# Landing tiles and the place of the high part in the last feed-forward of a transformer kernel

## The chip, the cores and the metric

The kernel runs on one core of a Trainium2 chip. The metric is the device time of one execution in microseconds (us); less is better. The engines are called PE (TensorE), DVE (VectorE), ACT (ScalarE), POOL (GpSimd) and SP (SyncE); each works through a queue of its own in order, and they wait for each other by semaphores.

## The reference

Input x is 8 x 1024 x 256 in float32. Four residual sublayers follow one another, each on a layer norm of x over the 256 features:

```
x = x + attention(layernorm(x))          # 2 heads of 128, rotary, causal softmax
x = x + ffn(layernorm(x))
x = x + linear_attention(layernorm(x))   # 8 heads of 64, decayed state, gated
x = x + ffn(layernorm(x))

ffn(x): gate = x @ (w_gate/127).T ; up = x @ (w_up/127).T      # 256 -> 768, integer weights
        return (silu(gate) * up) @ (w_down/127).T              # 768 -> 256
```

The change concerns the last line, the second use of ffn.

## The kernel before

x stays in the on-chip memory for the whole program (tile X, 64 tiles of 128 tokens). The program has four phases: attention, feed-forward 1 (ff1), linear attention, feed-forward 2 (ff2). Both feed-forwards come from one function, `feed_forward_phase` (line 954), called with nth = 1 or 2. Matmuls take operands that are split into a high part (rounded to float32r) and a low part (what is left), each used in a matmul of its own.

A feed-forward works in 16 units of 512 tokens. A unit has six steps f = 0 to 5, one for each 128 hidden features. In step f PE makes the gate projection (four matmuls 128x512, L1169) and the up projection (four more), then the down projection of the step three before (eight matmuls 128x256, L1178), which for f < 3 belongs to the unit before. ACT makes silu of the gate (L1106) and the high part of h of the step before (L1094). DVE makes h = silu * up (L1141), the low part of h of the step before (L1125), and besides: at f = 0 the statistics for the unit after next, at 1 their aggregation (L140), at 2 the residual of the unit before (L1132), at 3 the normalise of the unit after next (L156, four tiles), at 4 its block transpose (L256, `dve_blocks`).

The normalised units must be transposed for PE. DVE's block transpose turns squares of 32 x 32, and SP then moves the squares to their places with sixteen DMAs (`sp_move`, L271) into a landing tile. ACT makes the high part of what has landed (`act_high`, L276), POOL the low part (`pool_low`, L281), and PE waits for the low part (`pe_wait`) before the last down projection of the unit ahead. So in unit u: DVE normalises and transposes blocks of unit u + 2, SP moves unit u + 1, ACT and POOL make the two parts of unit u + 1. High and low parts have two tiles each, for even and odd units (`front.parts`: ln_xh, ln_xl and ff_odd_xh, ff_odd_xl). The landing tile is one, `raw`, in both feed-forwards. The tile of the blocks (ln_xn, upper half) is one too: DVE's transpose of unit u + 2 waits until unit u + 1 has landed (L255).

The order on each engine is written out by hand in the four functions `unit(u, par, first, left)`; par is the parity of the unit, `left` is 2 while two or more units follow, 1 in unit 14, 0 in unit 15. A `Signal` counts; `at(turn, k)` is the value after k events of that turn, and `at(u, 0)` is thus what the turn before has reached. SP's waits ahead of a move are, at line 1040 and in `sp_move`:

```
wait_alone(sp, front.lo_done.sem, front.lo_done.at(u, 1), front.sp_passed)
wait_alone(sp, self.blocks_done.sem, self.blocks_done.at(unit, 1), self.sp_passed)
```

On SP, after the move of unit u + 1, ff2 stores the result of unit u - 1 to memory (`store`, L1053). PE waits for h of three steps ago before a gate projection (three PSUM banks each for gate and up) and for the low part of a step before its down projection (`ready_for`, `down`). The chip runs the branch with terms = 2: the low parts of the integer weights are zero.

Of the kernel before, what the change touches and what calls it, by code (L numbers as in the profile page):

```python
# [13 lines left out]
F32 = mybir.dt.float32  # L14
# [7 lines left out]
P = 128  # L22
# [200 lines left out]
class Turned:  # L223
# [34 lines left out]

    def landing(self, par, raw):

        return self.raw[:] if raw else self.parts[par][1][:].bitcast(F32)

    def sp_move(self, sp, unit, par, raw=False):

        wait_alone(sp, self.blocks_done.sem, self.blocks_done.at(unit, 1), self.sp_passed)
        lo = self.landing(par, raw)
        for r in range(NQ):
            for c in range(NQ):
                src = self.blocks[r * SQ:(r + 1) * SQ, c, :].rearrange("p (n b) -> p n b", b=SQ)
                dst = lo[c * SQ:(c + 1) * SQ].rearrange("p k (t r b) -> p (k t) r b", t=UT, r=NQ)[:, :, r, :]  # L270
                sp.dma_start(dst, src).then_inc(self.landed.sem, 16)  # L271

    def act_high(self, act, unit, par, raw=False):
        hi, lo = self.parts[par]
        act.wait_ge(self.landed.sem, self.landed.at(unit, 16 * MOVES))
        self.nc.scalar.activation(hi[:], self.landing(par, raw), ACT.Copy).then_inc(self.hi_done.sem, 1)  # L276

    def pool_low(self, pool, unit, par, raw=False):
        hi, lo = self.parts[par]
        pool.wait_ge(self.hi_done.sem, self.hi_done.at(unit, 1))  # L280
        self.nc.gpsimd.tensor_tensor(lo[:], self.landing(par, raw), hi[:].bitcast(F32),  # L281
                                     ALU.subtract).then_inc(self.lo_done.sem, 1)
# [670 lines left out]
def feed_forward_phase(nc, block, sems, env, io, name, nth, front, following, signals):  # L953
# [5 lines left out]
    with ExitStack() as ctx:  # L959
# [21 lines left out]
        sx = [front.pair(0), front.pair(1)]  # L981
        NH = 4
        h_hi, h_lo = sb("h_hi", [P, NH, UN], F32R), sb("h_lo", [P, NH, UN], F32R)
        LAG = 3

        prep_hi, prep_lo = signals.prep_hi, signals.prep_lo
# [42 lines left out]
        @block.sync  # L1029
        def _(sp):  # L1030

            def unit(u, par, first, left):
                upcoming = next_of(u, par, left)
                if upcoming:
                    nfront, nu, npar = upcoming
                    if left:
                        if first:
                            sp.wait_ge(*env["a_scores_end" if nth == 1 else "lin_decayed_end"])
                        else:
                            wait_alone(sp, front.lo_done.sem, front.lo_done.at(u, 1), front.sp_passed)  # L1040
                    else:
                        wait_alone(sp, up_ready.sem, up_ready.at(u - 1, NF), front.sp_passed)
                    nfront.sp_move(sp, nu, npar, raw=bool(left))
                if following and isinstance(u, int) and u == 1:
                    sp.wait_ge(prep_lo, 2)
                    load_lin_weights(sp, env, io)
                if not following and not first:
                    store(u - 1)

            def store(u):  # L1050
                wait_alone(sp, x_done.sem, x_done.at(u, 1), front.sp_passed)
                at = bass.ds(u * UT, UT)
                sp.dma_start(out_v[:, at, :], X[:, at, :]).then_inc(stored, 16)  # L1053

            run_units(sp, unit, 1)
            if not following:
                store(NU - 1)
                sp.wait_ge(stored, 16 * NU)

        @block.gpsimd  # L1060
        def _(pool):

            def unit(u, par, first, left):
                upcoming, after = next_of(u, par, left), after_next(u, left)
                if first and nth == 1:
                    pool.wait_ge(*env["a_out_end"])
                    nc.gpsimd.tensor_copy(w_lo, stage[:, 0:NW]).then_inc(prep_lo, 2)
                if first and nth == 2:
                    pool.wait_ge(*env["lin_decayed_end"])
                    raw, hi = stage[:, parts_of_w[2]], w_hi[:, parts_of_w[2]]  # L1070
                    for f in range(NF):
                        at = slice(f * M, (f + 1) * M)
                        last = nc.gpsimd.tensor_tensor(lo_of_down[:, at], raw[:, at], hi[:, at].bitcast(F32), ALU.subtract)
                    last.then_inc(prep_lo, 1)
                if after and not first:
                    after[0].ln.pool_rstd(pool, after[1])
                if upcoming:
                    nfront, nu, npar = upcoming
                    nfront.pool_low(pool, nu, npar, raw=bool(left))

            def lin_low(n):
                at = bass.ds(n * LIN_PIECE, LIN_PIECE)
# [7 lines left out]
        def _(act):  # L1090
# [5 lines left out]
            def unit(u, par, first, left):  # L1096
                upcoming = next_of(u, par, left)
                for f in range(NF):
                    if f == (2 if first else NF - 2) and upcoming:
                        nfront, nu, npar = upcoming  # L1100
                        if left and not first:
                            act.wait_ge(up_ready.sem, up_ready.at(u - 1, NF))
                        nfront.act_high(act, nu, npar, raw=bool(left))
                    act.wait_ge(gate_ready.sem, gate_ready.at(u, f + 1))
                    act.wait_ge(h_done.sem, h_done.at(u, f - NB_GU + 1))
                    nc.scalar.activation(silu[:, f % NB_GU, :], PS[:, f % NB_GU, :], ACT.Silu,  # L1106
# [723 lines left out]
```

## Time and profile before

| | us |
|---|---|
| median of 3 runs | 1916.81 (1914.27 to 1918.74) |
| the profiled execution, own time | 1915.64 |
| its span | 1913.9 |
| granted TensorE clock, mean share | 0.998 |

The page gives for each engine its busy time in the span; the timelines give single instructions with start, length, engine, line, operation and, in brackets, how long the engine had been idle before and what it waited for. Starts count from the span's start. ff2's projections on PE run from 1618 us to the end.

### The profile page before, as it was taken

How to read it: one execution, taken by the hardware profiler on the slowest of the kernel's cores; microseconds unless marked ns; L12 is line 12 of the kernel's file. 1: busy time of each engine (PE TensorE's matmuls, PEld its weight loads, DVE VectorE, ACT ScalarE, POOL GpSimd, SP SyncE). 2: the span in 40 equal slices, each digit the busy share in tenths (PEclk: the TensorE clock that was granted, in tenths of full speed). 3: DMA queues.
4: the chain of work that ended last, by engine and by line, in shares of the span. 5: the costliest groups of instructions: out<-in, count | busy, mean ns of one | idle time of the engine just before them, and what ended most of it. 6: DMA issues, size and time to landing. Idle time of an engine off the chain costs nothing.

```text
span 1913.9 us, 36549 instructions
## 1 busy us (share of the span) xinstructions
PE 1875.6 (98%) x12321; PEld 1620.0 (85%) x12321; DVE 1325.4 (69%) x3141; ACT 879.4 (46%) x1716; POOL 519.6 (27%) x453
## 2 busy tenths in 40 slices
PE   7999999999999999999999999999999999899998
PEld 6888888888788888888888888888888887788887
DVE  6666566655677888766666666676667677778885
ACT  6666656665644444453333333333333332444443
POOL 5313202320321232132322222222222223422210
PEclk9999999999999999999999999999999999999999
DMA  7100000000022112220000000000000001222332
GB/s 251 33 1 0 0 0 0 0 0 0 12 63 46 29 29 32 34 66 12 13 10 10 9 9 9 10 11 11 11 11 11 12 12 18 38 62 62 64 59 53
DMA packets 230614, 53.19 MB, mean 28 GB/s; under 512 B 209680, under 2 KB 228752, under 8 KB 230160
## 3 DMA queue, kind: packets, MB, share of 16 engines
q1 hardware_dynamic: 229280, 49.53, 12.8%
q10 hardware_dynamic: 1264, 2.76, 0.4%
q8 instruction: 39, 0.64, 0.1%
q14 instruction: 31, 0.25, 0.0%
HBM read 18.69 MB, written 8.39 MB: 14 GB/s over the span
## 4 chain that ended last, share of the span: by engine, by line
PE 89%; DVE 4%; issue 2%; SPq 2%; POOL 1%; ACT 1%; DMA 0%; ACTq 0%; DVEq 0%; POOLq 0%
PE PS L323 18%; PE PS L1169 16%; PE PS L1178 9%; PE PS L332 7%; PE PS L855 7%; PE PS L826 6%; PE PS L1633 5%; PE PS L1675 4%; PE PS L1619 3%; PE PS L844 3%; PE PS L1652 3%; PE PS L866 2%; PE PS L1639 2%; SPq L271 2%; PE PS L1607 1%
## 5 line engine op out<-in xcount | busy, mean ns | idle before, releaser
L323 PE MATMUL PS<-ln_xh,lin_w 128*128 128x512 f32 x768 | 248.8, 392 | 0.0
L1106 ACT ACTIVATE ff_silu<-PS 128x512 f32<-128x512 f32 x192 | 114.5, 597 | 235.2 <-PE PS L1169 207.1
L1390 POOL TENSOR_TENSOR lin_yg_lo<-stage,lin_yg_hi 128x512 fp32r<-128x512 f32 x64 | 82.3, 1286 | 484.1 <-ACT lin_yg_hi L1408 484.1
L1141 DVE SCALAR_TENSOR_TENSOR ff_h<-PS,ff_silu 128x512 f32<-128x512 f32 x192 | 131.3, 685 | 111.3 <-PE PS L1169 93.5
L1408 ACT ACTIVATE lin_yg_hi<-stage 128x512 fp32r<-128x512 f32 x64 | 40.5, 632 | 347.0 <-DVE stage L1503 315.7
L323 PEld LDWEIGHTS PS<-ln_xh,lin_w 128*128 128x128 f32 x768 | 144.2, 188 | 28.7
L1125 DVE TENSOR_TENSOR ff_h_lo<-ff_h,ff_h_hi 128x512 fp32r<-128x512 f32 x192 | 168.2, 876 | 0.4
L564 POOL TENSOR_TENSOR qk<-qk,swapped 64x128 f32<-64x128 f32 (+2 forms) x96 | 96.5, 1005 | 243.0 <-DVE swapped L708 237.2
L1465 DVE TENSOR_TENSOR lin_AD<-PS,lin_decay 128x512 f32<-128x512 f32 x128 | 82.2, 684 | 104.6 <-PE PS L1619 104.6
L855 PE MATMUL PS<-probT,v_a 128*128 128x128 f32 x1152 | 153.4, 278 | 0.0
L855 PEld LDWEIGHTS PS<-probT,v_a 128*128 128x128 f32 x1152 | 139.5, 192 | 14.4 <-ACT probT L628 7.4
L323 PE MATMUL PS<-ln_xl,lin_w 128*128 128x512 f32 x384 | 150.0, 391 | 0.0
L826 PE MATMUL PS<-qk 128*128 128x512 f32 (+3 forms) x384 | 145.1, 489 | 0.9 <-POOL qk L564 0.9
L718 DVE TENSOR_REDUCE neg_max<-PS 128x1 f32<-128x256 f32 (+7 forms) x128 | 95.7, 753 | 64.3 <-PE PS L829 62.9
L1633 PE MATMUL PS<-lin_v,lin_AD 128*128 128x65 f32 x1024 | 133.4, 273 | 2.2 <-DVE lin_y L1478 2.2
L1633 PEld LDWEIGHTS PS<-lin_v,lin_AD 128*128 128x128 f32 x1024 | 124.2, 191 | 8.4 <-DVE lin_AD L1465 2.3
L1094 ACT ACTIVATE ff_h_hi<-ff_h 128x512 fp32r<-128x512 f32 x192 | 119.5, 623 | 10.9 <-DVE ff_h L1141 10.9
L167 POOL TENSOR_SCALAR ln_var_eps<-ln_mean_var 128x4 f32<-128x4 f32 x64 | 14.7, 229 | 360.4 <-DVE ln_mean_var L140 360.4
L1493 DVE SCALAR_TENSOR_TENSOR lin_state<-lin_state,lin_decay_c,PS 64x65 f32<-64x65 f32 x384 | 107.5, 280 | 7.0 <-PE PS L1652 2.9
L1178 PE MATMUL PS<-lin_w,ff_h_hi 128*128 128x256 f32 x384 | 97.9, 288 | 7.8 <-issue 5.8
L1178 PE MATMUL PS<-ff_w_hi,ff_h_hi 128*128 128x256 f32 x384 | 97.9, 288 | 4.4 <-DVE ff_h_lo L1125 1.9
L618 ACT ACTIVATE prob<-PS,neg_max 128x256 f32<-128x256 f32 (+7 forms) x128 | 94.5, 738 | 14.6 <-DVE neg_max L718 11.5
(172 smaller groups left out, 5183.8 us busy)
## 6 DMA issues: line engine op xcount, KB each, us to landing
ff_raw<-ln_xn SPq DMA_DIRECT2D x480, 32.0 KB, 2.0
ln_xl<-ln_xn SPq DMA_DIRECT2D x288, 32.0 KB, 1.9
out_x<-X SPq DMA_DIRECT2D x16, 512.0 KB, 2.9
X<-in_x SPq DMA_DIRECT2D x7, 1024.0 KB, 5.5
stage<-in_w_lin SPq DMA_DIRECT2D x1, 2048.0 KB, 8.2
stage<-in_w_gate SPq DMA_DIRECT2D x2, 768.0 KB, 7.4
stage<-in_w_up SPq DMA_DIRECT2D x2, 768.0 KB, 8.9
stage<-in_w_down SPq DMA_DIRECT2D x2, 768.0 KB, 10.2
```

What stands on the lines that cost most here:

```text
L323: last = nc.tensor.matmul(out, w, x, start=n == 0, stop=n == len(terms) - 1)
L332: last = nc.tensor.matmul(out, x[:, at], w, start=n == 0, stop=n == len(terms) - 1)
L826: last = nc.tensor.matmul(bank[:, 0:w], qk[:, 0, h, i * P:(i + 1) * P], qk[:, 1, h, c:c + w], start=True, stop=not diag)
L855: last = nc.tensor.matmul(O, V[:, j, h * DA:(h + 1) * DA], probT[:, n % 2, j, :], start=j == 0, stop=j == i)
L1094: nc.scalar.activation(h_hi[:, slot(par, f), :], h[:, f % 2, :], ACT.Copy).then_inc(hi_done.sem, 1)
L1106: nc.scalar.activation(silu[:, f % NB_GU, :], PS[:, f % NB_GU, :], ACT.Silu, scale=W_SCALE).then_inc(silu_done.sem, 1)
L1125: nc.vector.tensor_tensor(h_lo[:, slot(par, f), :], h[:, f % 2, :], h_hi[:, slot(par, f), :].bitcast(F32), ALU.subtract).then_inc(lo_done. ...
L1141: nc.vector.scalar_tensor_tensor(h[:, f % 2, :], PS[:, NB_GU + f % NB_GU, :], W_SCALE, silu[:, f % NB_GU, :], ALU.mult, ALU.mult).then_inc ...
L1169: ins = nc.tensor.matmul(PS[:, bank, :], w, x, start=n == 0, stop=n == len(parts) - 1)
L1178: ins = nc.tensor.matmul(Y[:, t // 2, (t % 2) * M:(t % 2 + 1) * M], a[:, slot(par, f), t * P:(t + 1) * P], w[:, f % NF, :], start=f == 0 a ...
L1493: last = nc.vector.scalar_tensor_tensor(S[rows, j, cols], S[rows, j, cols], Gc[rows, j:j + 1], new, ALU.mult, ALU.add)
L1633: last = nc.tensor.matmul(bank[:, hh * VA:(hh + 1) * VA], AD[:, ch % 2, hh % 2, 2 * g + hh // 2, :], v[:, c, HG * g + hh, :], start=hh == ...
```

## The change

In ff2 alone (nth = 2) a second landing tile raw2 is added; even units land in it, odd ones in raw. SP's first wait ahead of a move asks for the low part of unit u - 1 in place of unit u (`at(u, 2 - nth)`). ACT makes the high part of the next unit at step NF - 1 - nth, which is 3 in place of 4; in ff1 it is 4 as before. With the high part, POOL's low part is released a step sooner. Unit 0 keeps its step 2, and its SP wait is of another kind and stays.

```diff
--- before.py
+++ after.py
@@ -258,9 +258,9 @@
 
     def landing(self, par, raw):
 
-        return self.raw[:] if raw else self.parts[par][1][:].bitcast(F32)
-
-    def sp_move(self, sp, unit, par, raw=False):
+        return self.parts[par][1][:].bitcast(F32) if raw is None else raw
+
+    def sp_move(self, sp, unit, par, raw=None):
 
         wait_alone(sp, self.blocks_done.sem, self.blocks_done.at(unit, 1), self.sp_passed)
         lo = self.landing(par, raw)
@@ -270,12 +270,12 @@
                 dst = lo[c * SQ:(c + 1) * SQ].rearrange("p k (t r b) -> p (k t) r b", t=UT, r=NQ)[:, :, r, :]
                 sp.dma_start(dst, src).then_inc(self.landed.sem, 16)
 
-    def act_high(self, act, unit, par, raw=False):
+    def act_high(self, act, unit, par, raw=None):
         hi, lo = self.parts[par]
         act.wait_ge(self.landed.sem, self.landed.at(unit, 16 * MOVES))
         self.nc.scalar.activation(hi[:], self.landing(par, raw), ACT.Copy).then_inc(self.hi_done.sem, 1)
 
-    def pool_low(self, pool, unit, par, raw=False):
+    def pool_low(self, pool, unit, par, raw=None):
         hi, lo = self.parts[par]
         pool.wait_ge(self.hi_done.sem, self.hi_done.at(unit, 1))
         self.nc.gpsimd.tensor_tensor(lo[:], self.landing(par, raw), hi[:].bitcast(F32),
@@ -981,6 +981,7 @@
         sx = [front.pair(0), front.pair(1)]
         NH = 4
         h_hi, h_lo = sb("h_hi", [P, NH, UN], F32R), sb("h_lo", [P, NH, UN], F32R)
+        raws = (sb("raw2", [P, KT, UN]), front.raw) if nth == 2 else (front.raw, front.raw)
         LAG = 3
 
         prep_hi, prep_lo = signals.prep_hi, signals.prep_lo
@@ -1037,10 +1038,10 @@
                         if first:
                             sp.wait_ge(*env["a_scores_end" if nth == 1 else "lin_decayed_end"])
                         else:
-                            wait_alone(sp, front.lo_done.sem, front.lo_done.at(u, 1), front.sp_passed)
+                            wait_alone(sp, front.lo_done.sem, front.lo_done.at(u, 2 - nth), front.sp_passed)
                     else:
                         wait_alone(sp, up_ready.sem, up_ready.at(u - 1, NF), front.sp_passed)
-                    nfront.sp_move(sp, nu, npar, raw=bool(left))
+                    nfront.sp_move(sp, nu, npar, raw=raws[npar][:] if left else None)
                 if following and isinstance(u, int) and u == 1:
                     sp.wait_ge(prep_lo, 2)
                     load_lin_weights(sp, env, io)
@@ -1076,7 +1077,7 @@
                     after[0].ln.pool_rstd(pool, after[1])
                 if upcoming:
                     nfront, nu, npar = upcoming
-                    nfront.pool_low(pool, nu, npar, raw=bool(left))
+                    nfront.pool_low(pool, nu, npar, raw=raws[npar][:] if left else None)
 
             def lin_low(n):
                 at = bass.ds(n * LIN_PIECE, LIN_PIECE)
@@ -1096,11 +1097,11 @@
             def unit(u, par, first, left):
                 upcoming = next_of(u, par, left)
                 for f in range(NF):
-                    if f == (2 if first else NF - 2) and upcoming:
+                    if f == (2 if first else NF - 1 - nth) and upcoming:
                         nfront, nu, npar = upcoming
                         if left and not first:
                             act.wait_ge(up_ready.sem, up_ready.at(u - 1, NF))
-                        nfront.act_high(act, nu, npar, raw=bool(left))
+                        nfront.act_high(act, nu, npar, raw=raws[npar][:] if left else None)
                     act.wait_ge(gate_ready.sem, gate_ready.at(u, f + 1))
                     act.wait_ge(h_done.sem, h_done.at(u, f - NB_GU + 1))
                     nc.scalar.activation(silu[:, f % NB_GU, :], PS[:, f % NB_GU, :], ACT.Silu,
```

How the order moves on ACT, in ff2, unit 2 (first the silu of a step, L1106, then the high part of h of the step before, L1094; L276 is the high part of the next unit). Before:

```order
736 L1106 ACTIVATE ff_silu<-PS 128x512 [waits ff2_h_done,ff2_gate_ready]
737 L1094 ACTIVATE ff_h_hi<-ff_h 128x512 [waits ff2_down_done,ff2_h_done]
738 L1106 ACTIVATE ff_silu<-PS 128x512 [waits ff2_h_done,ff2_gate_ready]
739 L1094 ACTIVATE ff_h_hi<-ff_h 128x512 [waits ff2_down_done,ff2_h_done]
740 L276 ACTIVATE ff_odd_xh<-ff_raw 128x1024 [waits ff2_landed,ff2_up_ready]
741 L1106 ACTIVATE ff_silu<-PS 128x512 [waits ff2_h_done,ff2_gate_ready]
742 L1094 ACTIVATE ff_h_hi<-ff_h 128x512 [waits ff2_down_done,ff2_h_done]
```

After the change:

```order
736 L1107 ACTIVATE ff_silu<-PS 128x512 [waits ff2_h_done,ff2_gate_ready]
737 L1095 ACTIVATE ff_h_hi<-ff_h 128x512 [waits ff2_down_done,ff2_h_done]
738 L276 ACTIVATE ff_odd_xh<-ff_raw 128x1024 [waits ff2_landed,ff2_up_ready]
739 L1107 ACTIVATE ff_silu<-PS 128x512 [waits ff2_h_done,ff2_gate_ready]
740 L1095 ACTIVATE ff_h_hi<-ff_h 128x512 [waits ff2_down_done,ff2_h_done]
741 L1107 ACTIVATE ff_silu<-PS 128x512 [waits ff2_h_done,ff2_gate_ready]
742 L1095 ACTIVATE ff_h_hi<-ff_h 128x512 [waits ff2_down_done,ff2_h_done]
```

L276 stood between the high part of step 2 and the silu of step 4; it now stands one pair sooner, ahead of the silu of step 3.

DVE's order in ff2 is the same before and after but for line numbers one higher. Here it is before, in the second unit of the loop's body, from h of step 3 to the transpose of the unit after next:

```order
1075 L1141 SCALAR_TENSOR_TENSOR ff_h<-PS,ff_silu 128x512 [waits ff2_h_lo_done,ff2_silu_done,ff2_up_ready]
1076 L1125 TENSOR_TENSOR ff_h_lo<-ff_h,ff_h_hi 128x512 [waits ff2_down_done,ff2_h_hi_done]
1077 L156 TENSOR_SCALAR ln_xn<-X,ln_mean_var,ln_rstd 128x8x32 [waits ff2_ln_rstd_done]
1078 L156 TENSOR_SCALAR ln_xn<-X,ln_mean_var,ln_rstd 128x8x32 x3
1079 L1138 REGISTER_ALU
1080 L1141 SCALAR_TENSOR_TENSOR ff_h<-PS,ff_silu 128x512 [waits ff2_h_lo_done,ff2_silu_done,ff2_up_ready]
1081 L1125 TENSOR_TENSOR ff_h_lo<-ff_h,ff_h_hi 128x512 [waits ff2_down_done,ff2_h_hi_done]
1082 L255 ISA [waits ff2_ln_ready]
1083 L256 STREAM_TRANSPOSE ln_xn<-ln_xn 128x1024 [waits ff2_landed]
```

Nothing moved here; between h of step 3 and the transpose stand a low part, the normalise, h of step 4 and another low part.

## Rows read from the trace of the kernel before

**Rows 1.** The page: span and busy time by engine.
```profile
span 1913.9 us, 36549 instructions
...
PE 1875.6 (98%) x12321; PEld 1620.0 (85%) x12321; DVE 1325.4 (69%) x3141; ACT 879.4 (46%) x1716; POOL 519.6 (27%) x453
```

**Rows 2.** Chain that ended last, unit 15: start us, us, what.
```profile
1887.83 1.84 PE PS L1169 x8
...
1901.80 1.84 PE PS L1169 x8
```

**Rows 3.** Timeline of PE, starts of units 2, 7 and 8: start us, us, engine, line.
```profile
1662.77 0.40 PE L1169 MATMUL PS<-ln_xh,lin_w 128*128 128x512 f32 x1
...
1749.34 0.40 PE L1169 MATMUL PS<-ff_odd_xh,lin_w 128*128 128x512 f32 x1
...
1766.49 0.40 PE L1169 MATMUL PS<-ln_xh,lin_w 128*128 128x512 f32 x1
```

**Rows 4.** Timeline of ACT, 1756 to 1780 us; in brackets idle before.
```profile
1756.55 0.62 ACT L1094 ACTIVATE ff_h_hi<-ff_h 128x512 fp32r<-128x512 f32 x1
...
1761.83 1.06 ACT L276 ACTIVATE ln_xh<-ff_raw 128x1024 fp32r<-128x1024 f32 x1 [1.86 <-DMA ff_raw<-ln_xn]
1762.80 0.58 ACT L1106 ACTIVATE ff_silu<-PS 128x512 f32<-128x512 f32 x1
...
1778.91 1.06 ACT L276 ACTIVATE ff_odd_xh<-ff_raw 128x1024 fp32r<-128x1024 f32 x1 [1.80 <-DMA ff_raw<-ln_xn]
```

**Rows 5.** Timeline of DVE, 1763 to 1780 us.
```profile
1763.46 0.69 DVE L1141 SCALAR_TENSOR_TENSOR ff_h<-PS,ff_silu 128x512 f32<-128x512 f32 x1 [1.12 <-PE PS L1169]
1764.07 1.85 DVE L1125 TENSOR_TENSOR ff_h_lo<-ff_h,ff_h_hi 128x512 fp32r<-128x512 f32 x1
1765.84 1.23 DVE L256 STREAM_TRANSPOSE ln_xn<-ln_xn 128x1024 f32<-128x1024 f32 x1
...
1774.72 0.68 DVE L1125 TENSOR_TENSOR ff_h_lo<-ff_h,ff_h_hi 128x512 fp32r<-128x512 f32 x1
...
1778.11 1.38 DVE L156 TENSOR_SCALAR ln_xn<-X,ln_mean_var,ln_rstd 128x256 f32 x4
```

**Rows 6.** Timeline of POOL, unit 7.
```profile
1762.97 2.40 POOL L281 TENSOR_TENSOR ln_xl<-ff_raw,ln_xh 128x1024 fp32r<-128x1024 f32 x1 [5.67 <-ACT ln_xh L276]
```

**Rows 7.** Timeline of SP, the move of unit 9.
```profile
1767.17 10.40 SPq L271 DMA_DIRECT2D ff_raw<-ln_xn  x16
```

**Rows 8.** Waits of SP, 1732 to 1852 us (seven units): us, times, longest.
```profile
SPq L83 <- POOL ff_odd_xl L281: 15.3, 4, 4.0
SPq L83 <- POOL ln_xl L281: 12.2, 3, 4.1
SPq L83 <- DVE ln_xn L256: 11.1, 7, 1.6
```

**Rows 9.** Timelines of SP, DVE, POOL and ACT, units 0 to 2.
```profile
1618.97 35.52 SPq L271 DMA_DIRECT2D ff_raw<-ln_xn  x32
...
1635.83 1.23 DVE L256 STREAM_TRANSPOSE ln_xn<-ln_xn 128x1024 f32<-128x1024 f32 x1
...
1640.84 2.33 POOL L281 TENSOR_TENSOR ff_odd_xl<-ff_raw,ff_odd_xh 128x1024 fp32r<-128x1024 f32 x1
...
1657.49 3.54 DVE L156 TENSOR_SCALAR ln_xn<-X,ln_mean_var,ln_rstd 128x256 f32 x4
...
1676.12 1.06 ACT L276 ACTIVATE ff_odd_xh<-ff_raw 128x1024 fp32r<-128x1024 f32 x1 [2.72 <-PE PS L1169]
```

**Rows 10.** Timelines of ACT and PE, end of unit 14.
```profile
1882.99 1.06 ACT L276 ACTIVATE ff_odd_xh<-ff_raw 128x1024 fp32r<-128x1024 f32 x1 [1.86 <-DMA ff_raw<-ln_xn]
...
1886.64 0.36 PE L1178 MATMUL PS<-lin_w,ff_h_hi 128*128 128x256 f32 x1 [0.16 <-issue]
```

**Rows 11.** Busy time by stretch; columns to PEclk, the granted clock.
```profile
1639.00:1643.30 4.30, 0.12 (x2) 0.06 (x1) 4.17 (x4) 0.63 (x1) 4.17 (x4) 1.00 0.00 0
1643.30:1648.00 4.70, 4.70 (x19) 3.98 (x20) 0.42 (x1) 1.11 (x2) 0.00 (x0) 0.64 0.23 34
```

## The prediction

> **What bounds the kernel now.** I read the page first. TensorE (PE) is busy 98% of the span [rows 1]. A reader could stop there and call the kernel PE-bound. In the last feed-forward (ff2) that is nearly true and not quite, and the difference decides this case, so I went on to the timelines of the engines.
>
> PE's own pace comes from unit 15, which has no next unit to prepare. From its first to its last step 13.97 us pass for five steps [rows 2], 2.79 us a step, so six steps are 16.77 us. But unit 7 starts at 1749.34 and unit 8 at 1766.49 [rows 3]: 17.15 us. Something slower than PE sets the pace of the inner units by about 0.4 us.
>
> It is a closed loop through the other engines. Follow one turn from start to start. ACT makes the high part of unit 8 at 1761.83, having stood 1.86 us for the landing, and the silu of step 4 starts 0.97 later, at 1762.80 [rows 4]. DVE's product h of step 4 starts 0.66 later, at 1763.46; the low part of step 3 0.61 later; the block transpose (L256) of the unit after next 1.77 later, at 1765.84 [rows 5]. SP begins its sixteen DMAs 1.33 after that, at 1767.17, and issues them for 10.40 us [rows 7]. ACT takes the next landing at 1778.91 [rows 4], 1.34 after the last issue. The sum is 0.97 + 0.66 + 0.61 + 1.77 + 1.33 + 10.40 + 1.34 = 17.08 us. There is no slack in it: each member starts when the one before allows it. The low part takes 1.85 us there and 0.68 elsewhere [rows 5], because POOL's low part of the next unit runs from 1762.97 to 1765.37 [rows 6].
>
> **The change part by part.** The first feed-forward, attention and linear attention keep their instructions: for nth = 1 both index formulas give the old numbers and both landings are the same tile. Cost nothing. The added tile takes memory and no instruction. Every count of instructions stays (16 moves per unit, one high and one low part).
>
> *SP's weaker wait.* SP no longer waits for the low part of unit u, only for that of u-1, before it waits for the blocks. The view of SP's waits says what this is worth: seven times SP waited for POOL's low part and then, all seven times, 11.1 us in total, 1.59 us more each for DVE's transpose [rows 8]. The blocks are always last, and the blocks are not sooner by this edit. So in the steady units it is worth nothing. There is one exception. At the start SP issued two moves in a stretch that ends at 1654.49 [rows 9]; the second, 10.40 long, thus began at about 1644.1, since it waited for POOL's low part of unit 1 (1640.84 + 2.33 = 1643.17), though its blocks were done at 1637.06. It can now begin at 1637.2, 6.9 us sooner. ACT then finds unit 2 landed at step 3 of unit 1, POOL is done before DVE's normalise there, and that takes 1.38 us [rows 5] instead of the 3.54 it took while POOL ran [rows 9]. Against this DVE's low part, just before, is held some 0.3 us. The first fully exposed landing (ACT at 1676.12 [rows 9]) comes about 1.8 us sooner: -1.8 us.
>
> *The high part a step sooner.* This is the dear part. On ACT the high part now stands ahead of the silu of step 3. Were its data there, it would be free: in the unit that starts at 1749.34 ACT has done the work ahead of it by 1757.17 (7.83 us into the unit), but the landing is taken at 1761.83 (12.49 into it) [rows 3, 4]. ACT takes its queue in order, so it waits, and what queues behind it is now the silu of step 3, the high part of step 2, and everything DVE makes of them. The added members of the loop are those DVE has in order between h of step 3 and h of step 4. The new turn, from the start of the high part: silu of step 3 (0.97), h of step 3 (0.66), low part of step 2 (0.61), which meets POOL at the same offset as now and so is held alike (1.77), then the normalise of four tiles (1.38, less 0.07 of overlap: 1.31), h of step 4 (0.61 to the next start), low part of step 3 unheld (0.60: 0.68 less overlap), transpose to SP (1.33), 10.40, 1.34. That is 17.08 + 1.31 + 0.61 + 0.60 = 19.60 us, 2.52 more. The silu and high part that h and low part of those steps want are ready: ACT ends them some 2.6 and 3.2 us after the high part starts, and DVE comes to h of step 4 at 5.3.
>
> Can a head start save it? Only at first: landing 3, at 1676.12 - 1.8 = 1674.3, comes 11.5 us into unit 2, which starts at 1662.77 [rows 3], and ACT would be free at 7.8, so it waits already. Each turn takes 19.60 while PE would turn in some 17, so the lateness grows by 2.5 us a unit, and within two or three units PE itself stands at the end of step 5. There it needs the next unit's low part (1.14 + 2.40 us after the high part starts) and the low part of h of step 2, which ends 0.97 + 0.66 + 0.61 + 1.85 = 4.09 us after it. The second is later, by 0.5 us. PE's other waits are met: h of step 4 is done 6.0 us after the high part starts, and PE wants it at 4.1 + 0.1 + 1.05 (down projection) + 1.84 (first projections of the next unit [rows 2]) = 7.1. From then on the pace is the loop's.
>
> From the exposed landing at 1676.12 [rows 9] to the last at 1882.99 [rows 10] there are twelve turns: 12 x 2.52 = +30.2 us. Before, PE went on 3.65 us after the last landing (1886.64 [rows 10]); now 4.2: +0.5. The sum is 30.2 + 0.5 - 1.8 = +28.9 us.
>
> *The clock of PE.* Each unit now holds a pause of 19.6 - 16.8 = 2.8 us. After the pause of 4.2 us that ended at 1643.3 the granted clock was 0.64 over the next 4.7 us [rows 11], a part of it at 1.2 GHz instead of 2.4: 0.36 x 4.7 = 1.7 us lost. If every pause cost this, PE would still reach the end of step 5 1.1 us before it may go on. I count 0; the upper bound is in the range through the dearer case.
>
> The Trainium skill ("Trainium Kernel Development and Optimization", Best Practices) says to double-buffer so that DMA overlaps compute. By that rule the second landing tile lengthens the time in which a transfer may lie beside work, and the time would be that of the faster rival below; by the row of SP's waits [rows 8] the landing tile is not what SP waits for last. The row decides.
>
> **The sum.** The profiled execution took 1915.64 us (span 1913.9), so 1944.5 by its terms. It is 1.2 below the median of the three runs shown, 1916.81; between the two, I say 1945.0.
>
> **The rivals.**
>
> *Cheaper loop (0.12).* If the low part of step 2 were not held by POOL, the turn would be 1.17 shorter: 12 x (2.52 - 1.17) + 0.5 - 1.8 = +15 us, 1931. Against it: POOL starts 1.14 us after the high part, the low part of h 2.24 after it, in the new order as in the old [rows 4 to 6]. The Trainium skill ("SBUF — State Buffer", the section on its two separate sides) says the port pair that VectorE and GpSimd share is held by one of them for a whole instruction, the other blocked; by that this rival is out.
>
> *Dearer loop (0.13).* The normalise too meets POOL (3.54 for 1.38 [rows 5, 9], +2.16, less what the low part then saves, 1.17), or the pauses' slower clock delays gates that a silu waits for. One such microsecond a turn is +12 us, 1957.
>
> *Faster (0.07).* The loop is opened: the landing comes before ACT wants it, so high and low part lie under steps 3 and 4, POOL no longer holds the low part ahead of the transpose, and PE runs at its own pace. Then thirteen units save up to 0.38 us each (17.15 - 16.77), 5 us: 1912. This is what happens if landings come by 7.8 us into a unit. For it: the transpose would come about 1.8 us sooner once POOL is out of its way, as in unit 1. Against it: the landing stands at 12.5, the ten microseconds of issue stay, and landing 3 with all the head start still comes at 11.5.
>
> *No change (0.04).* DVE's idle time swallows the added members, and the turn stays at 17.1. DVE does stand 1.12 us before h of step 4 [rows 5], but it stands there because ACT and PE are not further; time before the landing does not shorten what comes after it. 1917.
>
> **How the numbers follow.** The forecast itself has 0.64. A measurement of this kernel tells about 0.2% (4 us) from no change. Slower: 0.64 + 0.12 + 0.13 = 0.89. Same: 0.04. Faster by more than 0.2%: 0.07. The range reaches from just under the cheaper loop to the dearer one, 1929 to 1957; outside it are the faster and the unchanged case and a part of the dearer.
>
> **What would show it.** Right: in ff2 the L276 rows on ACT lie 19.6 us apart in place of 17.1, each with some 6 to 7 us of idle time before it put to the DMA; SP waits for the transpose alone, for longer; PE has a pause of 2 to 3 us a unit ahead of a down projection, put down to DVE's low part; the busy share of PE in the last fifth of the span falls to about 86%; units of ff1 keep 17.1. Wrong: L276 with no idle time before it, or turns at 17.1, would say that the loop was not the pace-setter; turns well over 20 us, that a wait was added which I do not have.

## The result and the profile after

| | before | after |
|---|---|---|
| median of 4 runs each, us | 1915.99 (1914.27 to 1918.74) | 1944.01 (1942.90 to 1944.97) |
| span of the profiled execution, us | 1913.9 | 1941.4 |
| granted TensorE clock, mean share | 0.998 | 0.994 |

The ratio after to before is 1.0148, with a 95% interval of 1.0136 to 1.0160: 28 us slower. Line numbers of the changed kernel are one higher than before from the new line on. The page of the kernel after, its span, busy times and the chain by engine and by line, answers to [rows 1].

```profile
span 1941.4 us, 36549 instructions
...
PE 1883.1 (97%) x12321; PEld 1626.4 (84%) x12321; DVE 1318.3 (68%) x3141; ACT 878.0 (45%) x1716; POOL 523.8 (27%) x453
...
PE 80%; DVE 6%; SPq 6%; issue 3%; DMA 1%; ACT 1%; POOL 1%; ACTq 0%; DVEq 0%; POOLq 0%
```

The counts of instructions are those of before. The page alone says little, since 97% in place of 98% for PE would hardly alarm anyone. The chain does: SP's queue now has 6% of the whole span and PE 80%. The chain line of the page before reads:

```profile
PE 89%; DVE 4%; issue 2%; SPq 2%; POOL 1%; ACT 1%; DMA 0%; ACTq 0%; DVEq 0%; POOLq 0%
```

In the stretch from 1700 to 1760 us alone, the chain of the kernel after has no matmul in it at all. This is its summary by line:

```profile
by line: SPq L271 46.8%; issue 13.5%; DVE ff_h_lo L1126 12.5%; DMA ff_raw<-ln_xn 9.7%; DVE ln_xn L256 7.8%; DVE ln_xn L156 5.7%; ACT ff_silu L1107 2.9%; DVE ff_h L1142 0.8%; DVEq L1139 0.4%; DVEq L1141 0.2%; ACTq L1094 0.2%; ACTq L1106 0.1%
```

The same stretch of the kernel before is PE alone:

```profile
by line: PE PS L1169 64.4%; PE PS L1178 35.9%; issue 0.0%
```

In this stretch the loop through ACT, DVE and SP is now the only thing that sets the pace. Here is one turn of it. ACT's timeline after, 1750 to 1772 us, answers to [rows 4]:

```profile
1752.00 1.06 ACT L276 ACTIVATE ff_odd_xh<-ff_raw 128x1024 fp32r<-128x1024 f32 x1 [6.50 <-DMA ff_raw<-ln_xn]
1752.97 0.58 ACT L1107 ACTIVATE ff_silu<-PS 128x512 f32<-128x512 f32 x1
...
1771.60 1.06 ACT L276 ACTIVATE ln_xh<-ff_raw 128x1024 fp32r<-128x1024 f32 x1 [5.05 <-DMA ff_raw<-ln_xn]
```

DVE's timeline after, same turn ([rows 5]):

```profile
1753.63 0.69 DVE L1142 SCALAR_TENSOR_TENSOR ff_h<-PS,ff_silu 128x512 f32<-128x512 f32 x1 [5.90 <-ACT ff_silu L1107]
1754.24 1.81 DVE L1126 TENSOR_TENSOR ff_h_lo<-ff_h,ff_h_hi 128x512 fp32r<-128x512 f32 x1
1755.98 1.37 DVE L156 TENSOR_SCALAR ln_xn<-X,ln_mean_var,ln_rstd 128x256 f32 x4
1757.27 0.68 DVE L1142 SCALAR_TENSOR_TENSOR ff_h<-PS,ff_silu 128x512 f32<-128x512 f32 x1
1757.88 0.67 DVE L1126 TENSOR_TENSOR ff_h_lo<-ff_h,ff_h_hi 128x512 fp32r<-128x512 f32 x1
1758.47 1.23 DVE L256 STREAM_TRANSPOSE ln_xn<-ln_xn 128x1024 f32<-128x1024 f32 x1
```

SP's timeline after ([rows 7]):

```profile
1759.81 10.43 SPq L271 DMA_DIRECT2D ff_raw<-ln_xn  x16
```

From 1752.00 to 1771.60 pass 19.60 us. The normalise, one h and one low part now stand between the landing and the transpose. What used to be a wait of ACT of 1.86 us for the landing is 5.0 to 6.5 us in these units. The view of waits after, 1700 to 1850 us (us, times, longest), shows who stands for it; the last line is SP's own queue, 1732 to 1852 us ([rows 8]):

```profile
DVE ff_h L1142 <- ACT ff_silu L1107: 38.4, 7, 5.9
...
ACT ff_odd_xh L276 <- DMA ff_raw<-ln_xn: 24.5, 4, 6.5
...
ACT ln_xh L276 <- DMA ff_raw<-ln_xn: 23.1, 4, 6.5
...
PE PS L1179 <- DVE ff_h_lo L1126: 14.0, 7, 2.4
```

```profile
SPq L83 <- DVE ln_xn L256: 47.6, 6, 8.1
```

SP waited 38.6 us in seven units before the change, 27.5 of them put to POOL; now it waits 47.6 in six units, all for the transpose. Freed of one wait, it stands longer in the next.

### The profile page after: what moved, and what is told of

The parts are those of the page before. It is cut to its first block, busy times and chain, and to the rows that moved or that the text cites. A ratio compares the mean times of both kernels' runs of the same rounds, so it can differ in the third digit from the quotient of the medians.

```text
span 1941.4 us, 36549 instructions
## 1 busy us (share of the span) xinstructions
PE 1883.1 (97%) x12321; PEld 1626.4 (84%) x12321; DVE 1318.3 (68%) x3141; ACT 878.0 (45%) x1716; POOL 523.8 (27%) x453
## 3 DMA queue, kind: packets, MB, share of 16 engines
q1 hardware_dynamic: 229280, 49.53, 12.6%
## 4 chain that ended last, share of the span: by engine, by line
PE 80%; DVE 6%; SPq 6%; issue 3%; DMA 1%; ACT 1%; POOL 1%; ACTq 0%; DVEq 0%; POOLq 0%
PE PS L323 18%; PE PS L1170 10%; PE PS L332 7%; PE PS L855 7%; PE PS L826 6%; SPq L271 6%; PE PS L1179 6%; PE PS L1634 5%; PE PS L1676 4%; PE PS L1620 3%; PE PS L844 3%; PE PS L1653 3%; PE PS L866 2%; DVE ff_h_lo L1126 2%; PE PS L1640 2%
## 5 line engine op out<-in xcount | busy, mean ns | idle before, releaser
L1179 PEld LDWEIGHTS PS<-lin_w,ff_h_hi 128*128 128x128 f32 x384 | 75.1, 196 | 43.6 <-issue 15.3
```

Of the source, the lines that this page charges most:

```text
L1179: ins = nc.tensor.matmul(Y[:, t // 2, (t % 2) * M:(t % 2 + 1) * M], a[:, slot(par, f), t * P:(t + 1) * P], w[:, f % NF, :], start=f == 0 a ...
```

## The experiments

Each kernel below was timed beside the kernel before on the same chip; ratios are to it. "Turn" is the distance from one L276 of ff2 to the next on ACT, in the stretch from 1715 to 1790 us.

**Two tiles alone.** The change, with the high part back at step 4.

```diff
-                    if f == (2 if first else NF - 1 - nth) and upcoming:
+                    if f == (2 if first else NF - 2) and upcoming:
```

> Two landing tiles and SP's weaker wait alone; the high part stays at step 4 in ff2. My theory (the pace of a unit is the loop transpose, sixteen DMAs, high part, silu, h, low part, transpose; 17.08 us before, 19.60 after): SP's removed wait never ended last in the steady units, so turns between high parts (L276) stay at 17.1 us and the time is that of before within 0.2% (-2 to +1 us, ratio 0.999 to 1.0005). Rival (the tiles or the earlier DMAs cost time, or the landings collide with other work): ratio near 1.015, turns over 18 us. Rival (two tiles free the loop): turns under 16.95 us, 4 to 5 us faster.

Measured: 1915.40 us beside 1915.22, ratio 1.0001 [0.9991, 1.0010]. ACT's timeline of this kernel:

```profile
1744.03 1.06 ACT L276 ACTIVATE ff_odd_xh<-ff_raw 128x1024 fp32r<-128x1024 f32 x1 [1.84 <-DMA ff_raw<-ln_xn]
1761.16 1.06 ACT L276 ACTIVATE ln_xh<-ff_raw 128x1024 fp32r<-128x1024 f32 x1 [1.84 <-DMA ff_raw<-ln_xn]
```

The turn is 17.1 and the wait for the landing 1.84, both as before. With the high part at its old step, the second tile and the weaker wait are worth nothing that the interval of 0.1% to either side could tell. The rule to double-buffer that the prediction weighed (the Trainium skill, "Trainium Kernel Development and Optimization", Best Practices) has no gain to show here, for in the steady units the buffer was not what a transfer waited for last.

**The step alone.** The kernel before, one landing tile, old wait, with the high part at step 3.

```diff
-                    if f == (2 if first else NF - 2) and upcoming:
+                    if f == (2 if first else NF - 1 - nth) and upcoming:
```

> One landing tile and SP's old wait; the high part at step 3 in ff2. My theory: the whole loss is here, turns 19.6 us, PE pauses of about 2.5 us a unit, and the time is +28 to +31 us on before (ratio 1.0145 to 1.0165), as slow as the full change or up to 2 us slower. Rival (the loss comes from the second tile): no slower than before.

Measured: 1944.88, ratio 1.0150 [1.0133, 1.0167]. On ACT:

```profile
1755.51 1.06 ACT L276 ACTIVATE ff_odd_xh<-ff_raw 128x1024 fp32r<-128x1024 f32 x1 [5.01 <-DMA ff_raw<-ln_xn]
1775.11 1.06 ACT L276 ACTIVATE ln_xh<-ff_raw 128x1024 fp32r<-128x1024 f32 x1 [6.50 <-DMA ff_raw<-ln_xn]
```

A turn of 19.60 again. The loss is the step's: its ratio is that of the full change (1.0148) within the intervals, and the tiles alone stood at 1.0001.

**The normalise out of the loop.** The change, with ff2's normalise at DVE's step 2 instead of 3, so that it lies ahead of the landing.

```diff
-                        if f == (1 if first else 3):
+                        if f == (1 if first else 4 - nth):
```

> The full change, and in ff2 DVE normalises the unit after next at step 2 in place of 3, so that the normalise (1.31 us from start to start) leaves the loop. My theory: turns 19.60 - 1.31 = 18.3 us, twelve of them give back 15.7 us: about +12 us on before (ratio 1.006 to 1.007). Rival (the loss is ACT's wait as such, 6.5 us of idle in front of the high part, whatever DVE has between): turns stay at 19.6 us, ratio 1.015.

Measured: 1931.89, ratio 1.0088 [1.0071, 1.0105], 12.1 us less than the change. DVE's timeline, from h of step 3 on:

```profile
1750.67 0.69 DVE L1142 SCALAR_TENSOR_TENSOR ff_h<-PS,ff_silu 128x512 f32<-128x512 f32 x1 [3.56 <-issue]
1751.28 1.84 DVE L1126 TENSOR_TENSOR ff_h_lo<-ff_h,ff_h_hi 128x512 fp32r<-128x512 f32 x1
1753.25 0.69 DVE L1142 SCALAR_TENSOR_TENSOR ff_h<-PS,ff_silu 128x512 f32<-128x512 f32 x1
```

The turn is 18.53, where taking out 1.31 would give 18.29, and the ratio lies above the 1.006 to 1.007 that I had expected. The missing 0.24 stands in these rows: from the start of the held low part to the next member were 1.74 us in the change and are 1.97 here. That next member is now h, which has a semaphore wait on the low part that has just been made, and no other work lies between to cover it. That a member taken out gives back its length less what it covered is my reading of these rows; no run tests it by itself. The rival, a turn that stays at 19.6, is out: the normalise is a member of the loop.

**The transpose first.** The kernel before; in ff2 DVE transposes the blocks ahead of the low part of h in step 4, not behind it.

```diff
+                    if after and not first and f == 4 and nth == 2:
+                        after[0].dve_blocks(dve, after[1], (front, u + 1))
                     if f > 0 or not first:
                         low_part(u, par, f - 1)
...
-                        if f == (2 if first else 4):
+                        if f == (2 if first else 4) and (first or nth == 1):
```

> The kernel before, and in ff2 DVE's block transpose at step 4 goes ahead of the low part of step 3, which takes 1.77 us out of the loop: it could turn in 15.3 us, under PE's 16.8 to 16.9. My theory: turns fall to PE's pace, 16.8 to 17.0 us, and 2 to 5 us are gained (ratio 0.9975 to 0.999), less if the normalise now meets POOL's low part. Rival (PE sets the pace of before already): turns stay at 17.1, no gain.

Measured: 1910.81, ratio 0.9976 [0.9966, 0.9985]. A gain, from the same loop. Its turns alternate, 15.58 and 18.27. DVE's and then POOL's timeline, behind a landing that came at the end of a short turn (1758.52):

```profile
1759.57 3.60 DVE L156 TENSOR_SCALAR ln_xn<-X,ln_mean_var,ln_rstd 128x256 f32 x4
```

```profile
1759.66 2.39 POOL L281 TENSOR_TENSOR ln_xl<-ff_raw,ln_xh 128x1024 fp32r<-128x1024 f32 x1 [3.75 <-ACT ln_xh L276]
```

When a landing is in time, POOL's low part meets the normalise, whose four instructions then take 3.60 us in place of 1.38; the next transpose and landing are late by it, POOL then starts later and misses the normalise, and so on. The mean is 16.92 us.

Three more kernels ask what remains when the loop is short.

**The transpose first in both feed-forwards** (the edit above without its `nth` conditions).

> The kernel before, and the block transpose at step 4 ahead of the low part in both feed-forwards (the residual stays). My theory: ff1 has the same loop of 17.1 us as ff2 and gains about the same as ff2 did alone (4.4 us): 6 to 9 us faster than before, units of 16.9 us. Rival (ff1 is not bound by the loop): the 4.4 us of ff2 alone.

Measured: 1905.06, ratio 0.9948 [0.9933, 0.9964]. That is 10.4 us, a little more than the 6 to 9 expected. ff1 had the same loop: from its first landing taken from raw to the last pass 241.67 us here and 246.13 in the kernel before, 4.5 us less.

**The residual too.** In both feed-forwards, of the kernel before, residual and transpose ahead of the low part.

```diff
-                    if f > 0 or not first:
-                        low_part(u, par, f - 1)
                     if f == LAG - 1 and not first:
                         residual(u - 1, down_done.at(u, 0))
+                    if after and not first and f == 4:
+                        after[0].dve_blocks(dve, after[1], (front, u + 1))
+                    if f > 0 or not first:
+                        low_part(u, par, f - 1)
...
-                        if f == (2 if first else 4):
+                        if f == 2 and first:
```

> The kernel before, and on DVE in both feed-forwards the block transpose (step 4) and the residual (step 2) go ahead of the low part of that step. My theory: both loops run at PE's own pace, 16.77 us a unit, since PE no longer waits 0.15 us for the residual at step 3 nor for POOL at step 5: 0.36 us a unit in some 13 units of each of two feed-forwards, 8 to 11 us faster than before (ratio 0.9945 to 0.996). Rival (the low parts, later by 1.2 us, hold a down projection): turns over 17.1, no gain or slower.

Measured: 1902.85, ratio 0.9935 [0.9921, 0.9948]; the mean turn is 16.80 (its turns alternate too, 15.57 and 18.03). The gain of 12.6 us is above the 8 to 11 expected. The page hides why the residual matters. These are PE's first projection and its first matmul of the down projection in step 5 of unit 7 of the kernel before; the next unit starts at 1766.49 [rows 3]:

```profile
1763.45 0.40 PE L1169 MATMUL PS<-ff_odd_xh,lin_w 128*128 128x512 f32 x1
...
1765.43 0.39 PE L1178 MATMUL PS<-lin_w,ff_h_hi 128*128 128x256 f32 x1
```

In the kernel before PE is never idle in a unit, yet in step 3 of unit 7 the projections start 1.91 us ahead of the down projection, not 1.84, and that one takes 1.03 instead of 0.95: +0.15, the wait for the residual, gone here. In step 5 they read 1.98 and 1.06: +0.24, the wait for POOL's low part, which ends at 1765.37 [rows 6]. Together they are, to 0.01, the 0.38 by which a unit was above PE's own pace; with the transpose first 16.92 are left, with the residual too 16.80. The intervals of the kernel above (0.9948) and of this one (0.9935) overlap, so the residual's own share rests on the turns.

**Everything sooner.** The same order on DVE; in ff2 also the two tiles, the high part at step 3, the normalise at step 2 and the transpose at step 3.

> The order of b1 in ff1; in ff2 the full change (two landing tiles, high part at step 3) with DVE's side brought forward as well: normalise at step 2, transpose at step 3 ahead of the low part, residual ahead of the low part. My theory: the loop is then high part, silu, h, transpose, moves (15.3 us), so PE sets the pace in ff2 too and the high part at step 3 costs nothing: the time of b1 within 2 us. Rival (the high part at step 3 is dear in itself): slower than before.

Measured: 1909.59, ratio 0.9966 [0.9952, 0.9979], 6.7 us more than the kernel above: a miss. Its turn is 17.40. DVE's timeline:

```profile
1756.27 3.47 DVE L156 TENSOR_SCALAR ln_xn<-X,ln_mean_var,ln_rstd 128x256 f32 x4
...
1760.26 1.23 DVE L256 STREAM_TRANSPOSE ln_xn<-ln_xn 128x1024 f32<-128x1024 f32 x1
```

The high part a step sooner puts POOL's low part (1757.09, 2.50 us) right on the normalise in every unit of this stretch, and PE stands 0.40 us a unit for the low part of h behind it. So the place of the high part was undone alone:

**The same, with the high part back at step 4.**

```diff
-                    if f == (2 if first else NF - 1 - nth) and upcoming:
+                    if f == (2 if first else NF - 2) and upcoming:
```

> As the kernel with everything brought forward on DVE (ff2: two landing tiles, normalise at step 2, transpose at step 3, residual and transpose ahead of the low parts; ff1: transpose and residual ahead), but the high part of ff2 back at step 4. That kernel's turns were 17.4 us, with PE waiting 0.4 us a unit for the low part of step 2, behind the normalise that POOL's low part holds (3.47 us). My theory: with the high part a step later POOL's low part meets neither, and ff2 falls to PE's 16.8 us: the time of the kernel with only the DVE order changed (ratio 0.993 to 0.995). Rival (the loss against it comes from the normalise at step 2 or the transpose at step 3): ratio 0.9965 again.

Measured: 1901.66, ratio 0.9929 [0.9916, 0.9943], the lowest of all. This is 7 us below the kernel above by the ratios, so in this order too the high part costs something at step 3. ACT's timeline:

```profile
1733.19 1.05 ACT L276 ACTIVATE ff_odd_xh<-ff_raw 128x1024 fp32r<-128x1024 f32 x1
1749.97 1.05 ACT L276 ACTIVATE ln_xh<-ff_raw 128x1024 fp32r<-128x1024 f32 x1
1766.74 1.05 ACT L276 ACTIVATE ff_odd_xh<-ff_raw 128x1024 fp32r<-128x1024 f32 x1
```

DVE's timeline in the same unit:

```profile
1749.88 1.38 DVE L156 TENSOR_SCALAR ln_xn<-X,ln_mean_var,ln_rstd 128x256 f32 x4
...
1751.78 1.24 DVE L256 STREAM_TRANSPOSE ln_xn<-ln_xn 128x1024 f32<-128x1024 f32 x1
1752.93 1.14 DVE L1126 TENSOR_TENSOR ff_h_lo<-ff_h,ff_h_hi 128x512 fp32r<-128x512 f32 x1
```

POOL's and then SP's timeline:

```profile
1751.10 2.43 POOL L281 TENSOR_TENSOR ln_xl<-ff_raw,ln_xh 128x1024 fp32r<-128x1024 f32 x1 [3.69 <-ACT ln_xh L276]
```

```profile
1753.11 10.41 SPq L271 DMA_DIRECT2D ff_raw<-ln_xn  x16
```

No bracket stands behind L276: the landing is there before ACT wants it. The normalise is all but done as POOL starts (it ends 0.16 us later, at its 1.38), and only the end of POOL's work meets a low part of h; PE is at work in all of the 150 us from 1700 to 1850. The turn of 16.78 is PE's own pace. Here SP does use the second tile: its moves begin at 1753.11, while POOL reads the other tile until 1753.53. Yet the gain over one tile and the better order (0.9935) lies inside the intervals of both. With one tile this kernel's moves would start about 0.4 us later, and by my estimate still land some 1.5 us before ACT takes them (1753.53 + 10.41 + 1.34 = 1765.3 against 1766.74); no run tests that.

The last two kernels shorten the loop at its longest member, SP's issue, in the changed kernel.

**Half of the moves on ACT, in one piece.** SP issues eight of the sixteen, ACT the other eight behind the high part of its step 0 (ff2, units 1 to 14).

```diff
-            for c in range(NQ):
+            for c in cs:
...
+                    if nth == 2 and f == 0 and not first and left:
+                        nfront, nu, npar = upcoming
+                        wait_alone(act, front.lo_done.sem, front.lo_done.at(u, 0), act_passed)
+                        nfront.sp_move(act, nu, npar, raw=raws[npar][:], cs=range(2, NQ), passed=act_passed)
```

> The full change, and in ff2 units 1 to 14 SP issues eight of the sixteen moves and ACT the other eight, after the high part at step 0. My theory: the issue time of one queue, 10.40 us, is the largest member of the loop; halved, the loop could turn in 19.6 - 5.2 = 14.4 us, so PE sets the pace (16.8 to 17.0 us a unit) though the high part stands at step 3: 2 to 5 us faster than before (ratio 0.997 to 0.999), 32 us faster than the full change. Rival (the high part at step 3 costs by its place on ACT, not by the lateness of the landing): still 19 us or more a turn, ratio above 1.01. Second rival (5.2 us of DMA issue on ACT delays silu): turns between 17 and 19 us.

Measured: 1934.38, ratio 1.0095 [1.0080, 1.0111]. That is 9.6 us below the change, a part only of what the loop's arithmetic promised, and still slower than before: the second rival of the expectation came true. ACT's timeline:

```profile
1739.96 0.60 ACT L1109 ACTIVATE ff_silu<-PS 128x512 f32<-128x512 f32 x1 [1.75 <-PE PS L1176]
1740.42 0.61 ACTq L271 DMA_DIRECT2D ff_raw<-ln_xn  x1
...
1741.06 4.76 ACTq L271 DMA_DIRECT2D ff_raw<-ln_xn  x7
1746.00 0.60 ACT L1109 ACTIVATE ff_silu<-PS 128x512 f32<-128x512 f32 x1 [4.93 <-PE PS L1176]
...
1748.02 1.06 ACT L276 ACTIVATE ff_odd_xh<-ff_raw 128x1024 fp32r<-128x1024 f32 x1
```

and PE's long wait in the view of waits, 1700 to 1850 us:

```profile
PE PS L1185 <- DVE X L1139: 13.2, 8, 1.9
```

The landing is no longer late. But ACT cannot make the silu of step 1 while it issues: 6.04 us pass between two silus that PE feeds 2.79 apart. (The view puts the 4.93 us to PE, because issuing counts as idle; the rows between say what ACT did.) Through h and what DVE makes behind it, the residual last, this reaches PE as a pause of mostly 1.7 us, at most 1.9, and the turn is 18.7, which is 1.9 above PE's 16.8.

**The same moves on ACT, spread** as 3, 3 and 2 over its steps 0 to 2.

```diff
+                    if nth == 2 and f < 3 and not first and left:
...
+                        nfront.sp_move(act, nu, npar, raw=raws[npar][:], moves=range(8 + 3 * f, min(11 + 3 * f, MOVES)),
+                                       passed=act_passed, wait=f == 0)
```

> As the split of the moves before (the full change, eight moves on SP, eight on ACT in ff2 units 1 to 14), but ACT's eight are spread: three at step 0, three at step 1, two at step 2, so that no silu is held over 2 us. In the first split the turn was 18.7 us with no wait for the landing and a new wait of 1.7 us of PE for the residual, which I put down to ACT's five microseconds of issue in one piece. My theory: spread out, that wait goes, the landing comes by some 10.5 us into the unit, and the high part at step 3 costs nothing: units of 16.9 to 17.1 us, ratio 0.997 to 1.000. Rival (the issue of DMAs on ACT costs whatever its place, or the high part at step 3 does): turns over 18 us, ratio over 1.005.

Measured: 1909.87, ratio 0.9966 [0.9955, 0.9977]. ACT's timeline (the high part is L279 here):

```profile
1740.06 1.06 ACT L279 ACTIVATE ff_odd_xh<-ff_raw 128x1024 fp32r<-128x1024 f32 x1 [1.60 <-DMA ff_raw<-ln_xn]
...
1756.95 1.06 ACT L279 ACTIVATE ln_xh<-ff_raw 128x1024 fp32r<-128x1024 f32 x1 [1.58 <-DMA ff_raw<-ln_xn]
```

The turn is 16.89, and the change with this addition is 34 us below the change alone (1909.87 against 1944.01), though ACT still waits 1.6 us at step 3. So the step is not dear by itself; it is dear while the loop through SP's ten microseconds is longer than PE's unit. The Trainium skill ("Trainium Kernel Development and Optimization", Key Constraints) says that issuing DMAs from several engines saves only the issuing sequencer's time. Both runs agree, and that time, 5.41 us of SP's issue in place of 10.43, is what was wanted here: from issue to landing a move took 2.0 us in the median from SP and from ACT alike.

## Why the prediction was right

The forecast was 1945.0 us, the median is 1944.01, and the mechanism is the one that was forecast: the step, through the loop. The sum was made against the profiled execution, so its terms are compared with the profiled spans, 1913.9 and 1941.4. The landings that bound the stretches, on ACT's timeline after (the third and the last), answer to [rows 9] and [rows 10]:

```profile
1673.53 1.06 ACT L276 ACTIVATE ff_odd_xh<-ff_raw 128x1024 fp32r<-128x1024 f32 x1 [3.96 <-DMA ff_raw<-ln_xn]
...
1909.23 1.06 ACT L276 ACTIVATE ff_odd_xh<-ff_raw 128x1024 fp32r<-128x1024 f32 x1 [6.56 <-DMA ff_raw<-ln_xn]
```

| term | predicted | measured | from |
|---|---|---|---|
| twelve turns, landing 3 to 15 | +30.2 | +28.83 | 235.70 (1673.53 to 1909.23) less 206.87 (1676.12 to 1882.99) |
| landing 1 to landing 3 | -1.8 | -0.64 | 44.09 less 44.73 |
| last landing to PE's next down projection | +0.5 | +0.54 | 4.19 (1913.42) less 3.65 |
| from there to the end | 0 | +0.72 | 27.98 less 27.26 |
| all that lies ahead of landing 1 | 0 | -1.95 | 1629.44 in place of 1631.39 |
| sum | +28.9 | +27.5 | 1941.4 less 1913.9 |

That the sum is so near is in part luck: the terms miss by -1.4, +1.2, +0.7 and -1.95, and these cancel in part. The last is no effect of the change, which alters no instruction ahead of the first landing. In the profiled executions of the kernels that differ in ff2 alone this landing comes anywhere from 1629.44 (the change) to 1631.93 us.

*The loop.* The turn was forecast at 19.60 and is 19.60. The members agree one by one: 0.97, 0.66, 0.61, the held low part 1.74 (1.77), the normalise 1.29 (1.31), 0.61, 0.59 (0.60), 1.34 (1.33), 10.43 (10.40), and 1.36 (1.34) to the landing. That the step and not the tiles costs this is shown by the two kernels that carry one each; that the normalise is a member, by the kernel that takes it out.

*The twelve turns* came out 1.4 us lower. The turns after sum up to 235.70, 0.5 above 12 x 19.60, since the one in which the loop's exit lies took 20.12. The turns before sum up to 206.87, 1.9 above 12 x 17.08: its own exit turn took 18.47, 1.4 above 17.08, and the rest is that the others vary from 17.08 to 17.18. (The exit is where the program leaves its loop over the units, behind unit 12; this landing is taken in unit 13.) Before, SP had issued that turn's moves by 1863.18, but ACT took the landing 2.69 us later, not 1.34; after, the issue took 10.90 us, not 10.43. I counted neither, and that is the term's error; why the exit costs this is not shown.

*The start* gave a third of what was booked. SP did begin sooner: it issued 32 moves in 29.46 us, not 35.52, and the normalise of that unit took 1.37 us, not 3.54. The step that failed is that PE would come through unit 1 as fast as before. Landing 3 hangs on a transpose behind h of step 4 of that unit, and this h waited for PE. PE's first down projection behind its pause (1641.27) took 1.84 us in place of 1.15: the granted clock was 0.50 over the 4 us from there, and 0.60 over the 4 us behind the same pause before. Unit 2 starts 32.30 us after the first landing, not 31.38. These 0.92 us are most of the 1.16 that are missing. Both pauses were 4.18 us long; why the clock fell lower once is open.

*SP's weaker wait worth nothing* in the steady units, *the 0.5 us for the low part of step 2* and *the place of PE's pause* (a down projection, put to DVE's low part) came as written.

*ACT's wait* was to be some 6 to 7 us. It is 6.5 in most units and 5.0 in those whose start fell under a slow clock (the landings at 1712.81, 1771.60 and 1849.92), where PE fed ACT later.

*PE's busy share* was to fall to about 86% in the last fifth of the span. It reads 348.54 of 388.30 us from 1553.1 on, 90%, and 135.96 of 150 us from 1700 to 1850, 91%. I took 16.8 of work in 19.6. The gap is the way the pause is read: the full pauses are 2.4 us, not 2.8, since the residual's 0.15 us a unit is still there and matmuls' ends overlap the wait; after a slow clock PE is busy for longer and the next pause is 1.0; and the stretch from 1700 to 1850 holds seven pauses in 7.65 turns.

*The clock.* I counted it as hidden in the loop and it is: the turns stay at 19.6 whatever the clock did. What I did not count is the last pause, behind which there is no loop: the granted clock was 0.62 over 4 us there, 1.00 at the same place before, and the stretch to the end took 0.72 us more. No run separates the two. The granted clock in the 4 us behind twelve pauses, by stretches of the kernel after (columns: stretch, us, PE busy, PEclk, DMA share, GB/s):

```profile
1698.00:1702.00 4.00, 4.00 (x15) 0.57 0.00 0
1717.10:1721.00 3.90, 3.90 (x25) 1.00 0.00 0
1736.70:1741.00 4.30, 4.30 (x27) 1.00 0.00 0
1756.20:1760.00 3.80, 3.80 (x14) 0.57 0.00 0
...
1834.60:1838.60 4.00, 4.00 (x15) 0.58 0.00 0
...
1893.90:1898.00 4.10, 4.10 (x26) 1.00 0.00 0
1913.50:1917.50 4.00, 4.00 (x16) 0.62 0.02 4
```

*The rivals.* "Cheaper loop" fell by its own row: the low part was held for 1.81 us. "Dearer loop" named the normalise meeting POOL; it did not here (1.37), but it did in four of the experiments (3.46 to 3.60: the transpose first, in ff2 and in both, the residual too, and everything sooner), so the mechanism is real and only the place was missed. The Trainium skill ("SBUF — State Buffer", the section on its two separate sides) describes the shared port pair as an exclusive lock for a whole instruction, and both these rows and the low part's 1.81 beside 0.67 us agree. "Faster" needed landings by 7.8 us into a unit; the change never came near, but the kernel with the better order on DVE and the high part at step 4 has every landing in time and takes 1901.66 us.

## What to carry to other kernels

When several in-order engines pass work round in a circle, write one turn down from start to start and look which instructions stand in it; moving a waiting instruction ahead of others puts those others into the circle, whatever buffers are added. A second buffer can be worth something only where the buffer's wait is the one that ends last. Here that was so at the start of ff2, and in the steady units not before the transpose had been brought forward too (1753.11 against 1753.53). And a DMA issue is work of its engine: here sixteen of them were the longest member of the circle, and eight of them moved in one piece to an engine that computes saved 10 us, spread between its computations 34.

## What the runs showed of the hardware

The granted clock is not a function of the length of the pause before it alone. Of the nine pauses of 2.4 to 3.0 us from 1697 to 1913 us four were followed by some 4 us at 0.57 to 0.62 (1697, 1756, 1834, 1913), the mean of a stretch that was mostly at 1.2 GHz, and five by the full 2.4 GHz, the longest pause (3.00) among them. The pause after each of the first three was of only 0.93 to 1.01 us. Why these four is open; nothing in the rows read here tells them from the others.

What DVE loses to POOL depends on which instruction meets which: four normalise instructions took 3.46 to 3.60 us beside POOL's low part and 1.38 alone, while POOL's low part kept its 2.4 to 2.5 us, and which of DVE's instructions POOL meets can alternate from unit to unit and make a kernel's turns alternate with it, 15.58 and 18.27.

One of these DMAs takes its issuing engine about 0.65 us on SP (10.43 for sixteen) and 0.67 on ACT (5.36 for eight), and ACT began no silu in that time although it had one to make.
